# A graph kernel's edge pass: the first layer made turned, with its weights held in TensorE

## The reference

```
edge_index = stack([src, dst])
# layer 0, segments over edge_index[0]:
h   = relu(concat([x_i, x_j - x_i]) @ W + b)          # one row per edge
out = segment_max(h, tgt)
x   = layernorm(x + maximum(out, 0))
# layer 1: degrees, norm = D[row] * D[col], mean and std of x -> 6 coefficients (tiny MLP, softmax)
result = coeffs[0] * x
for k in 1..5:
    tx = segment_sum(norm * tx[col], row);  result += coeffs[k] * tx
x   = layernorm(x + result)
```

## Time and profile before

| what | value |
|---|---|
| median of the runs | 3210.05 us |
| profiled execution | 3222.55 us |
| its span | 3220.8 us |
| DVE busy over the span | 2484.1 us (77%) |
| POOL busy | 2209.6 us (69%) |
| ACT busy | 2048.2 us (64%) |
| PE busy | 1841.5 us (57%) |

### The profile page before, as it was taken

The page is one execution under the profiler, slowest core; times in us unless marked ns, Lnnn a source line. Parts: engine busy times, 40 slices in busy tenths (PEclk is TensorE's granted clock), DMA queues, the critical chain, the costliest instruction groups (busy, mean ns, idle before and its releaser), DMA issues. The chain is left out here.

```text
span 3220.8 us, 66969 instructions
## 1 busy us (share of the span) xinstructions
PE 1841.5 (57%) x9618; PEld 1106.1 (34%) x9618; DVE 2484.1 (77%) x11593; ACT 2048.2 (64%) x4831; POOL 2209.6 (69%) x2285
## 2 busy tenths in 40 slices
PE   7996666479999996888888883333333332000000
PEld 6884444345555553444444441111111111000000
DVE  8996999999999995888989986455556666555554
ACT  7995877468888883888888873264546401444443
POOL 6777777067777775677777765676666665777776
PEclk9998999889999995778878875555555555555555
DMA  4310444167777774788878875666667633222221
GB/s 143 110 25 20 117 114 114 47 171 212 210 215 214 216 205 100 199 208 202 214 199 216 216 187 125 162 187 181 175 154 207 161 91 79 69 70 68 73 74 53
DMA packets 736782, 467.28 MB, mean 145 GB/s; under 512 B 411287, under 2 KB 622546, under 8 KB 736728
## 3 DMA queue, kind: packets, MB, share of 16 engines
q1 hardware_dynamic: 636084, 321.23, 36.8%
q0 software_dynamic: 75296, 92.22, 12.6%
q10 hardware_dynamic: 25348, 53.33, 5.4%
HBM read 271.38 MB, written 197.86 MB: 146 GB/s over the span
## 5 line engine op out<-in xcount | busy, mean ns | idle before, releaser
L1708 POOL DMA_INDIRECT rows_H<-tab,at_H x424 | 403.9, 952 | 214.6 <-DVE at_H L1761 110.4
L1009 POOL DMA_INDIRECT rec<-edge_x,pos x392 | 394.1, 1005 | 151.0 <-issue 133.0
L1211 POOL DMA_INDIRECT rows_M<-x_ext,at_M x400 | 378.2, 946 | 170.1 <-issue 101.9
L1983 POOL DMA_INDIRECT out_x<-res_L,to_L x384 | 373.7, 973 | 118.7 <-issue 105.1
L1729 ACT ACTIVATE node_H<-node_H,mean,M2n 125x64 f32<-125x64 f32 x800 | 273.6, 426 | 256.6 <-issue 150.5
L1869 PE MATMUL zT_H<-ident,z_H 128*64 128x128 f32 x496 | 150.5, 407 | 444.4 <-issue 351.4
L903 PE MATMUL gps<-table,hiT 125*128 125x400 bf16 x1568 | 307.2, 334 | 1.9 <-ACT table L950 1.1
L380 POOL DMA_INDIRECT edge_x<-in_x,x_at x196 | 204.4, 1043 | 70.2 <-issue 58.8
L563 POOL DMA_INDIRECT edge_x<-in_x,x_at x196 | 189.5, 967 | 67.6 <-issue 59.4
L2000 ACT ACTIVATE std_L<-M_L,coef 128x2 f32<-128x2 f32 x192 | 56.7, 295 | 275.9 <-DVE M_L L2062 275.9
L368 DVE TENSOR_SCALAR ohc<-iota,lo 128x400 bf16<-128x400 f16 x784 | 216.7, 318 | 0.0
(11 more groups left out here) (346 smaller groups left out, 6217.7 us busy)
## 6 DMA issues: line engine op xcount, KB each, us to landing
tab<-given_M SPq DMA_DIRECT2D x98, 384.0 KB
hibc_f<-dst_hi_rows SPq DMA_DIRECT2D x98, 256.0 KB
hibc<-hi_rows SPq DMA_DIRECT2D x98, 256.0 KB
srcbc<-src_rows SPq DMA_DIRECT2D x98, 256.0 KB
tab<-given_M SPq DMA_DIRECT2D x98, 256.0 KB
own<-given_M SPq DMA_DIRECT2D x98, 256.0 KB
own_L<-own SPq DMA_DIRECT2D x192, 128.0 KB
x_ext<-wide SPq DMA_DIRECT2D x100, 241.5 KB
```

The source lines that it names most:

```text
L1009: pool.indirect_dma_start(out=d.rec, out_offset=bass.IndirectOffsetOnAxis(ap=pos[:, s, j:j + 1], axis=0), in_=edge_x[:, i + s * (EB // 2), ...
L1211: pool.indirect_dma_start(out=rows[:, s, j, :], out_offset=None, in_=d.x_ext, in_offset=bass.IndirectOffsetOnAxis(ap=at[:, s, j:j + 1], ax ...
L1708: pool.indirect_dma_start(out=rows[:, s, j, :], out_offset=None, in_=gather, in_offset=bass.IndirectOffsetOnAxis(ap=at[:, s, j:j + 1], axi ...
L1983: pool.indirect_dma_start(out=d.out, out_offset=bass.IndirectOffsetOnAxis(ap=to[:, s, j:j + 1], axis=0), in_=res[:, s, j, :], in_offset=No ...
```

## The change

The product of the first layer is made turned: `Wd`, padded with 64 columns of zeros in front (`WdP`, 128x128), is now the weights, and `best` is the moving operand, one matmul with 512 columns (`layer`). Its result goes into the upper half of `pT` of the same group, where the own rows stood before. DVE's `first_layer` reads it there and adds the own rows from the upper half of `best`; it writes the upper half of a new tile `both_T`, whose lower half is what was `sums`. One set of four 128x128 transposes (`both_back`) turns sums and rows together into `back`. ACT's `give_sums` copies both halves of `back` into `given`, and the row statistics and the layer norm read and write the rows there. `u` is gone.

Some waits go with it. `load_x` waits for `pT_done` instead of `u_done`. `layer` waits for the scans and for `pair_turned` of its group. `combine` waits for `u_done` of the group two before.

```diff
+            def layer(i, s):
+                settle(pe, k)
+                pe.wait_ge(max_done[s], i + 1)
+                pe.wait_ge(pairT_ready[s], i + 1)
+                pe.wait_ge(sum_done[s], i + 1)
+                pe.matmul(pT[s % 2][:], WdP[:], best[:, s], start=True, stop=True).then_inc(h_done[s], 1)
+
+            def both_back(i, s):
+                settle(pe, k)
+                pe.wait_ge(u_done[s], i + 1)
+                two_before(pe, i, s, far_back)
                 for j in range(GT):
-                    pe.matmul(back[s % 2][:, j, 0:C], best[:, s, j * P:(j + 1) * P], k.Wd[:], start=True, stop=True)
+                    last = pe.transpose(back[s % 2][:, j, :], both_T[:, s, j * P:(j + 1) * P], k.ident[:])
...
-                two_before(pe, i, s, pairT_ready)
-                two_before(pe, i, s, sum_done)
+                two_before(pe, i, s, u_done)
...
-            pipeline(pe, NG, NS, (4, LAST, product), (8, LAST, sum_rows), (3, LAST, turn), (5, LAST, best_back),
-                     (4, LAST, combine), (5, LAST, sums_back), (4, NG - 1, sum_chunk))
+            pipeline(pe, NG, NS, (6, LAST, both_back), (5, LAST, layer), (4, LAST, product), (8, LAST, sum_rows), (3, LAST, turn),
+                     (4, LAST, combine), (4, NG - 1, sum_chunk))
...
             def pair_turned(i, s):
                 act.wait_ge(pT_done[s], i + 1)
-                act.wait_ge(back_done[s], i)
+                act.wait_ge(u_done[s], i)
...
             def give_sums(i, s):
-                act.wait_ge(u_done[s], i + 1)
+                act.wait_ge(back_done[s], i + 1)
                 act.wait_ge(row_away[s], i * 48)
-                act.activation(far_sum[:, s], back[s % 2][:, :, C:2 * C], ACT.Copy).then_inc(far_back[s], 1)
+                act.wait_ge(row_summed[s], i)
+                act.activation(given[:, s, :, C:3 * C], back[s % 2][:], ACT.Copy).then_inc(far_back[s], 1)
...
-                    last = act.activation(row[:, s, j], u[:, s, j], ACT.Identity, scale=rstd[:, b, GT + j:GT + j + 1],
+                    last = act.activation(row[:, s, j], row[:, s, j], ACT.Identity, scale=rstd[:, b, GT + j:GT + j + 1],
...
+            dve.memset(WdP[:, 0:C], 0.0)
+            dve.tensor_copy(WdP[:, C:], k.Wd[:])
...
             def first_layer(i, s):
-                dve.wait_ge(back_done[s], i + 1)
-                dve.wait_ge(row_ready[s], i)
-                dve.scalar_tensor_tensor(u[:, s], back[s % 2][:, :, 0:C], 0.0, pair[:, s, :, C:2 * C], ALU.max, ALU.add
+                dve.wait_ge(h_done[s], i + 1)
+                dve.wait_ge(back_done[s], i)
+                dve.scalar_tensor_tensor(uT[:, s], pT[s % 2][C:, :], 0.0, best[C:, s], ALU.max, ALU.add
                                          ).then_inc(u_done[s], 1)
...
             def row_moments(i, s):
                 n, b = three_on(i, s)
-                dve.wait_ge(u_done[s], i + 1)
+                dve.wait_ge(far_back[s], i + 1)
                 for j in range(GT):
-                    dve.bn_stats(st[:, b, GT + j], u[:, s, j])
+                    dve.bn_stats(st[:, b, GT + j], row[:, s, j])
```

More of the change, by code:

```diff
@@ L1100, in edge_pass @@
         best = sb("best", [P, NS, GPOS])
-        sums = sb("sums", [C, NS, GPOS])
-        u = sb("u", [P, NS, GT, C])
+        both_T = sb("both_T", [P, NS, GPOS])
+        sums, uT = both_T[0:C], both_T[C:]
+        WdP = sb("WdP", [P, P])
         given = sb("given", [P, NS, GT, 3 * C])
@@ L1109, in edge_pass @@
         back = ps("back", [P, GT, P])
+        h_done = [sem(f"h_done{s}_M") for s in range(NS)]
         ids_in, x_in, chunk_in, ids_ready, gathered = slots("ids_in", "x_in", "chunk_in", "ids_ready", "gathered")
@@ L1180, in load_x @@
                 before, = settle(sp, k, i)
-                sp.wait_ge(u_done[s], before)
+                sp.wait_ge(pT_done[s], before)
                 sp.dma_start(pair[:, s, :, C:2 * C], d.rec[positions(i, s, 1), 0:C].rearrange("(j p) f -> p j f", p=P)
@@ L1259, in product @@
                 pe.matmul(vT[s % 2][:], k.Wb[:], xT[:, s % 2], start=True, stop=True).then_inc(vT_done[s], 1)
-            def best_back(i, s):
+            def layer(i, s):
                 settle(pe, k)
@@ L1264, in best_back @@
                 pe.wait_ge(pairT_ready[s], i + 1)
-                two_before(pe, i, s, u_done)
+                pe.wait_ge(sum_done[s], i + 1)
[3 more added lines that the diff above has]
+                pe.wait_ge(u_done[s], i + 1)
                 two_before(pe, i, s, far_back)
                 for j in range(GT):
-                    pe.matmul(back[s % 2][:, j, 0:C], best[:, s, j * P:(j + 1) * P], k.Wd[:], start=True, stop=True)
[L1270 to L1274, removed]
+                    last = pe.transpose(back[s % 2][:, j, :], both_T[:, s, j * P:(j + 1) * P], k.ident[:])
                 last.then_inc(back_done[s], 1)
@@ L1370, in _ @@
             act.wait_ge(begun, 1)
-            pipeline(act, NG, NS, (4, LAST, follow), (4, LAST, penalty), (4, LAST, far), (3, LAST, turned),
-                     (7, LAST, make_rows), (4, LAST, pair_turned), (6, LAST, give_sums), (3, NG, deviation))
+            pipeline(act, NG, NS, (6, LAST, give_sums), (4, LAST, follow), (4, LAST, penalty), (4, LAST, far), (3, LAST, turned),
+                     (7, LAST, make_rows), (4, LAST, pair_turned), (3, NG, deviation))
             all_squares(act)
@@ L1448, in running_max @@
                 dve.wait_ge(vT_done[s], i + 1)
-                dve.wait_ge(back_done[s], i)
+                dve.wait_ge(u_done[s], i)
                 dve.wait_ge(max_done[prev], i + 1 if s else i)
@@ L1475, in shifts @@
                                   ).then_inc(idle_ready[s], 1)
-            pipeline(dve, NG, NS, (1, NG - 1, target), (3, NG - 1, mark), (4, NG, inverse), (6, LAST, first_layer), (4, NG, shifts),
-                     (4, LAST, far_factors), (3, NG - 1, far_moments), (6, LAST, row_moments), (3, NG, chunk_moments),
-                     (3, NG, moments), (4, LAST, running_max), (4, LAST, running_sum))
+            pipeline(dve, NG, NS, (1, NG - 1, target), (3, NG - 1, mark), (4, NG, inverse), (4, NG, shifts),
+                     (4, LAST, far_factors), (3, NG - 1, far_moments), (5, LAST, first_layer), (6, LAST, row_moments),
+                     (3, NG, chunk_moments), (3, NG, moments), (4, LAST, running_max), (4, LAST, running_sum))
             link = Chain(dve, mch)
```

## The result

The changed kernel takes 3517.28 us (median of 4 runs, 3511.58 to 3521.03) against 3214.13 us before in the same comparison: a ratio of 1.0948, with an interval of 1.0908 to 1.0987. It is slower, by 303 us, where 194 were forecast, and outside the range (3290 to 3500).

A forecast was written before the change was run, and what follows sets the result against it. No single engine bound the edge pass at full clock; PE did at half clock. With 45% at half clock, 8.01 and 11.05 us give 9.14 a period, 2.00 more over 97 periods: 3210 + 194 = 3404 us, range 3290 to 3500.

The forecast's parts named there:

- The place: PE's order: `both_back` and `layer` directly ahead of `product` join a loop back to `cont`, lengthening the edge pass period.
- The loop over `pair_turned`: Edge pass: `cont`, ACT's list through `pair_turned`, `layer`, `product`, next `cont`; 8.01 us at full clock against 6.37.
- The first rival: Edge pass: the new loop binds but the clock stays full; +84 us, 3294 us; chance 0.10.
- the share of time at half clock: Edge pass: 40% of the time at half clock before, taken as 45% after because PE's gap before `combine` grows.
- the prediction's own mixture: Edge pass: full- and half-clock periods mixed by time, 1 / (0.55/8.01 + 0.45/11.05) = 9.14 us a period.
- the all-half chain of 11.05 us: Edge pass at half clock: `cont` to `combine`, `sum_chunk`, `both_back`, `layer`, `product`, next `cont`; 11.05 us against 8.80.
- The second rival: Edge pass: the clock is low three quarters of the time; 10.09 us a period, +286 us, 3496 us; chance 0.13.
- the prediction's signs of being wrong: Edge pass: `product` well before `pair_turned` ends, a full-clock period under 7, or half-clock share outside 0 to 75%.
- DVE's list would be 6.76 us: DVE in the edge pass: a longer `first_layer` adds 0.39 to 6.37 us at full clock, hidden under 8.01.
- The 6.37 us for before at full clock: Edge pass: one period of the kernel before at full clock, read from DVE's reciprocal in the timeline.
- The third rival: Edge pass: the new loop does not bind, edits only cost their work; 7.60 us a period, 3255 us; chance 0.04.
- the fourth: Edge pass: no binding loop, and the larger matmul keeps the clock up; 6.76 us a period, 3173 us; chance 0.03.

The follow-up runs named there:

- experiment 3: The kernel before with only `best_back` moved directly ahead of `product` in PE's list: 3523.0 us, ratio 1.0981.
- experiment 7: The kernel before with `best_back` directly ahead of `product`, plus eight matmuls of zeros ahead of `combine`: 3326.5 us, ratio 1.0357.
- experiment 2: The changed kernel with eight matmuls of zeros between `turn` and `combine`, nothing moved: 3294.0 us, ratio 1.0267.
- experiment 4: The kernel before with five matmuls of zeros between `best_back` and `combine`: 3188.3 us, ratio 0.9942.
- experiment 6: The changed kernel with `layer` ahead of `combine`, `first_layer` behind `moments` on DVE, and four matmuls of zeros between `layer` and `combine`: 3220.1 us, ratio 1.003.
- experiments 1 to 3: The first of them: the changed kernel with `layer` moved from ahead of `product` to directly ahead of `combine`: 3285.5 us, ratio 1.0242.
- Experiment 12: The changed kernel with `turn`'s four transposes issued three times over, eight more ahead of `combine`: 3294.3 us, ratio 1.0241.
- the fifth kernel: The changed kernel with `layer` directly ahead of `combine` and `first_layer` moved behind `moments` on DVE: 3221.4 us, ratio 1.002.
- the ninth: The kernel before with `sum_chunk` moved from behind `sums_back` to directly ahead of `combine`, nothing added: 3222.6 us, ratio 1.0033.
- experiment 10: The changed kernel with `sum_chunk` moved directly ahead of `combine`, nothing else: 3357.3 us, ratio 1.046.
- experiments 11 and 12: The first of them: the changed kernel with four matmuls of zeros between `turn` and `combine`: 3293.2 us, ratio 1.0256.
- experiment 8: The changed kernel with eight matmuls of zeros directly ahead of `both_back`, the gap ahead of `combine` left: 3565.8 us, ratio 1.1108.

## Why the prediction was wrong in size

**The place was right.** Both new steps lie on the loop, and order alone costs as much (experiment 3); that it is as much to within 13 us is in part luck, since that kernel's clock is lower and its `best_back` has a wait of its own (experiment 7). The loop over `pair_turned` was predicted at 8.01 us for full clock and measured at 7.84 with the wait named (experiment 2). The first rival, the loop at full clock, was priced at 3294 us; filled, the kernel takes 3294.0. That close it is luck: the loop is 0.17 us shorter than priced, 16 us over 97 periods, and the profiled execution of before, from which the 7.14 was read, is 15 us longer than the median of 3207 in that comparison.

**The step that failed is the share of time at half clock:** "I take a little more, 45%". It is 66%. The 40% of before was carried over to a loop with another wait, and no row gave the 5% on top. By the prediction's own mixture this alone makes 1 / (0.34/8.01 + 0.66/11.05) = 9.79 us a period instead of 9.14, and 3467 us, which is still inside the range. The other 0.38 us to 10.17, 37 us over 97 periods, is the second failure, the mixture itself: it lets the two clocks fall evenly over the period, as they did before, when full clock lasted several periods (1.00 from 1352 to 1382 us). Now the clock changes within each period, and the full third of the time lies where ACT is on the path and PE waits, so it buys little: of the all-half chain of 11.05 us, 10.25 are left. No run holds the changed kernel at half clock for a whole period, so the 11.05 itself is not measured; experiment 3's sum of that kind came true. The second rival, three quarters at half clock, came nearest in time (3496) with a share too high, by the same mixture. None of the prediction's signs of being wrong came up: the share is inside its 0 to 75%, and what it says of full and of half clock is said of periods at one clock, of which this kernel has none after its first groups.

**The sum, by the runs.** At full clock the change costs 3294 - 3188 = 106 us (experiments 2 and 4). About 30 of them stay with the order mended (experiment 6), where DVE never waits for another engine, so they are put down to its longer list. The half clock costs the changed kernel 3517 - 3294 = 223 us, and the kernel before 19 (3207 - 3188). This splits the loss and doesn't check it: 106 + 223 - 19 = 310 is 3517 - 3207 by construction, and differs from the 303 measured only by the median of before.

**The rest.** `first_layer` takes 0.69 us (0.75 taken) and `give_sums` 0.60, both off the path as said. That DVE's list would be 6.76 us was low: in experiment 6 it is 7.03, of which DVE is busy 528.28 / 550 x 7.03 = 6.75, and the other 0.28 are idle time between its instructions. A part of that may be latency: `shift` needs the reciprocal, and the `first_layer` that stood between them before filled that wait; this was not tried apart. The 6.37 us for before at full clock holds only in stretches: with full clock throughout it is 6.70 (experiment 4). The third rival fell with experiments 1 to 3; the fourth is nearest to experiment 6, which is not faster either.

**The rule on transposes.** The Trainium skill ("TensorE: Matmul & The Clock Gate", section "Part 4: PE-mode transpose") says that full clock doesn't engage for transposes and that they don't count as PE's work in the same way. Experiment 12 disagrees: with transposes alone added, the clock went from 0.67 to 1.00. The measurement decides.

**What stays open** is what exactly decides the clock in this stage. Added work in the gap always brought it to 0.98 or more. But the fifth kernel holds 1.00 with PE busy in 397 of 550 us, and the ninth stays at 0.80 with 533 of 600. A wait of about 1.3 us ahead of `combine` goes with 0.80 (before), 0.83 (experiment 10) and 1.00 (experiments 11 and 12), one of 2.20 us with 0.67 and with 0.82 (experiment 8). So neither PE's busy share nor the length of the gap ahead of `combine` alone explains all runs. That work added there ends the half clock is shown; why is not.

## What to carry to other kernels

When a step is moved on an in-order engine, write down the loop it joins: what it waits for, what stands behind it, and who waits for that; here one list entry was worth 232 us. Price it at both levels of TensorE's clock, and don't carry the old mixture over: here a new wait of PE changed when the clock falls, and full clock helps only where PE is on the path. A few matmuls of zeros in the wait are a cheap test of that, and here the kernel before with five of them is the fastest of all (3188 us).

## What was not expected of the hardware

- More work on PE made three kernels faster: eight matmuls of zeros took 223 us from the changed kernel and 197 us from that of experiment 3, five took 19 us from the one before.
- The granted clock can fall and rise once in each loop period, for hundreds of microseconds on end (0.67 on average over 1010 us), and be full for most of the time in which PE waits.
- Eight transposes a group hold the clock up as well as four bf16 matmuls of 512 columns.
